# Swin-style window attention in four layers, one core: PE's order within an attention slot, and two queues for the first loads and the last stores

## The reference

```python
h = norm(x)                          # L0: over the whole image; L1 to L3: over the channels of a token
h = roll(h, (-3, -3)); windows of 7 x 7 = 49 tokens
q, k, v = h @ qkv_w + qkv_b          # 12 heads of 8 channels in L0 to L2, 4 heads of 24 in L3
a = softmax(q * hd**-0.5 @ k.T + rel_bias + mask)
x = x + roll(window_reverse(a @ v @ proj_w + proj_b), (3, 3))
x = x + mlp(norm(x))                 # 96 -> 384 -> 96, GELU between; L3 has one more norm on the 384
```

## Time and profile before

| what | value |
|---|---|
| median of 3 runs | 10196.03 us (10195.53 to 10201.48) |
| the profiled execution | 10191.26 us |
| its span on the core | 10189.4 us, so 1.9 us lie around it |
| mean granted clock of TensorE | 0.972 of full |
| PE busy | 87% of the span |
| PE weight loads busy | 64% |
| DVE / ACT / POOL busy | 67% / 54% / 50% |
| DMA | 57.27 MB, mean 6 GB/s |

### The profile page before, as it was taken

One profiled execution on the slowest core, in us unless ns is written; L12 is line 12 of the kernel. 1 busy time (PEld: TensorE's weight loads), 2 busy tenths in 40 slices (PEclk: granted clock), 3 DMA queues, 4 the chain that ended last, 5 costly groups with the idle time before them and its releaser, 6 DMA issues.

```text
span 10189.4 us, 315201 instructions
## 1 busy us (share of the span) xinstructions
PE 8861.1 (87%) x110128; PEld 6488.0 (64%) x110128; DVE 6823.7 (67%) x19999; ACT 5520.1 (54%) x9632; POOL 5091.5 (50%) x6190
## 2 busy tenths in 40 slices
PE   1899898998889899899888989989888998989984
PEld 0666666765667666666566667666556666667653
DVE  3766767657776666766867676666687667676574
ACT  0655646455564655646556464554556556464552
POOL 4764545443475554544257454554427645454431
PEclk8999999999999999999999999999999999999997
DMA  2010000000001000000000100000000000000000
GB/s 32 6 20 5 0 1 0 1 1 0 3 6 28 14 1 1 0 1 0 0 5 11 30 5 1 1 1 1 0 1 6 20 4 0 1 0 1 1 0 19
DMA packets 177574, 57.27 MB, mean 6 GB/s; under 512 B 175987, under 2 KB 177020, under 8 KB 177107
## 3 DMA queue, kind: packets, MB, share of 16 engines
q1 hardware_dynamic: 167768, 50.63, 2.8%
q0 software_dynamic: 4880, 0.71, 0.1%
q10 hardware_dynamic: 4459, 0.12, 0.1%
HBM read 31.71 MB, written 19.27 MB: 5 GB/s over the span
## 4 chain that ended last, share of the span: by engine, by line
issue 37%; POOL 21%; PE 20%; DVE 11%; ACT 4%; DVEq 3%; POOLq 3%; ACTq 0%; DMA 0%
POOL masked_bias L447 7%; POOL S L461 5%; PE ps L761 4%; PE ps L784 4%; PE ps L704 3%; POOL rstd L435 3%; ACT PT L574 3%; DVE xn L939 2%; POOL xn L478 2%; POOL xn L483 2%; DVE bst L849 2%; PE ps L746 2%; DVE bst L1049 2%; DVEq L939 2%; PE ps L668 1%
## 5 line engine op out<-in xcount | busy, mean ns | idle before, releaser
L461 POOL TENSOR_TENSOR S<-S,mx 113x588 f32<-113x588 f32 (+1 forms) x2048 | 2064.3, 1008 | 2618.8 <-DVE mx L988 2617.8
L704 PEld LDWEIGHTS ps<-Vroom,PT 98*49 98x49 f32 x40960 | 1123.4, 127 | 1365.3 <-ACT PT L574 1197.2
L574 ACT ACTIVATE PT<-ps 98x588 f32<-98x588 f32 (+1 forms) x2048 | 1179.4, 576 | 1490.9 <-PE ps L746 1456.5
L704 PE MATMUL ps<-Vroom,PT 98*49 98x18 f32 (+1 forms) x40960 | 1339.0, 203 | 651.7 <-ACT PT L574 628.4
L986 DVE TENSOR_TENSOR S<-ps,bias 113x588 f32<-113x588 f32 (+1 forms) x1536 | 973.4, 634 | 981.9 <-PE ps L690 915.0
L530 ACT ACTIVATE room<-ps,kmask 96x392 f32<-96x392 f32 x2048 | 1191.3, 583 | 578.3 <-PE ps L660 578.3
L988 DVE TENSOR_REDUCE mx<-S 113x12 f32<-113x588 f32 (+1 forms) x2048 | 1359.5, 664 | 70.7
L746 PE MATMUL ps<-ident,S 113*98 113x113 f32 x10240 | 1348.9, 262 | 2.4 <-ACT S L550 2.3
L550 ACT ACTIVATE S<-S 113x588 f32<-113x588 f32 (+1 forms) x2048 | 1238.4, 605 | 56.2 <-POOL S L461 56.2
L761 PEld LDWEIGHTS ps<-w,G 128*98 128x98 f32 x12288 | 1139.1, 168 | 112.8 <-issue 61.1
L746 PEld LDWEIGHTS ps<-ident,S 113*98 113x98 f32 x10240 | 1067.1, 129 | 197.4 <-issue 191.4
(11 more groups left out here) (81 smaller groups left out, 11852.9 us busy)
## 6 DMA issues: line engine op xcount, KB each, us to landing
mask<-L_conv_mask_matrix_dram SPq DMA_DIRECT2D x256, 37.5 KB
x<-x_dram SPq DMA_DIRECT2D x64, 84.0 KB
out_dram<-x SPq DMA_DIRECT2D x64, 84.0 KB
x<-x_dram SPq DMA_DIRECT2D x240, 10.5 KB
out_dram<-x SPq DMA_DIRECT2D x240, 10.5 KB
x<-x_dram SPq DMA_DIRECT2D x192, 18.4 KB
out_dram<-x SPq DMA_DIRECT2D x192, 18.4 KB
x<-x_dram SPq DMA_DIRECT2D x64, 48.0 KB
```

Of the source, the lines that this page charges most:

```text
L461: pool.tensor_tensor(v, v, m, ALU.subtract).then_inc(a_sub, 1)
L574: act.activation(PT[:, e, 0:blocks, :, :].rearrange("p (b t) w n -> p b (t w) n", b=banks), PTps[:, 0:banks, 0:2 * k, 0:N], ACT.Copy).then ...
L704: last = pe.matmul(Ops[ROW2 * w:ROW2 * w + N, p, b, :], PT[:, s % 2, b, w, :], room_of[:, o if s < 2 else t, p, w, b, :], start=True, stop ...
```

## The change

It has two parts.

1. In PE's `attend`, the weighted sums of pair s-2 move from before the projections of a slot to after them. The order in a slot is then scores, projection, weighted sums, turning.
2. The first 228 loads are issued first of all, every other one by SP and by ACT. The clearing of `x` is gone, and the waits on it. DVE takes the statistics of the first group before it writes the bias tables. The last group's stores are cut in two halves of two images, 156 DMAs each: SP issues the first half when 16 of the last stage's 32 quads are done, and SP and ACT issue every other one of the second half when the last quad is done.

```diff
-        def runs():
+        def runs(first, last):
...
-                    rows = [(slice(0, IMGS * A), r + SHIFT)]
+                    rows = [(slice(first * A, last * A), first * H + r + SHIFT)]
...
-        def tokens(sp, g, store, s):
+        def tokens(eng, g, store, s, first=0, last=IMGS, turn=0, turns=1):
...
+            for n, (q, a, j, row, col) in enumerate(runs(first, last)):
+                if n % turns != turn:
+                    continue
...
         @block.sync
...
             nc.disable_value_cache = True
+            tokens(sp, 0, False, s_x, turn=0, turns=2)
             load(ident[:, :], d["ident"])
...
-            sp.wait_ge(s_memset, 2)
-            tokens(sp, 0, False, s_x)
+            sp.wait_ge(s_memset, 1)
             load(mask4[:, :, :].rearrange("p a b -> p (a b)"), d["mask4"])
...
             sp.sem_inc(s_next, 1)
+            sp.wait_ge(m_res, GROUPS * LAYER_QUADS - NQ // 2)
+            stand(sp)
+            tokens(sp, GROUPS - 1, True, s_out, 0, IMGS // 2)
             sp.wait_ge(s_fin, GROUPS)
-            tokens(sp, GROUPS - 1, True, s_out)
-            sp.wait_ge(s_out, GROUPS * (16 * TOK_DMAS))
+            tokens(sp, GROUPS - 1, True, s_out, IMGS // 2, IMGS, turn=0, turns=2)
+            sp.wait_ge(s_out, (GROUPS - 1) * (16 * TOK_DMAS) + 2 * 16 * HALF_DMAS)
...
         @block.scalar
         def _(act):
-            act.wait_ge(s_memset, 2)
+            tokens(act, 0, False, s_x, turn=1, turns=2)
+            act.wait_ge(s_memset, 1)
             load_bias(act, 0, s_braw0)
...
+            act.wait_ge(s_fin, GROUPS)
+            tokens(act, GROUPS - 1, True, s_out, IMGS // 2, IMGS, turn=1, turns=2)
...
         @block.tensor
...
                                 last.then_inc(a_sc, 1)
-                            if on(-1) if s < 2 else on(0):
-                                wait(a_pte, before)
-                                p = (s + 2) % 4
...
                             if s == 0 and on(-2):
                                 wait(a_ote, i - 2)
...
                                 last.then_inc(a_t1, 1)
+                            if on(-1) if s < 2 else on(0):
+                                wait(a_pte, before)
+                                p = (s + 2) % 4
+                                if s == 2:
+                                    wait(a_o, i - 1)
+                                    wait(a_v0e, i)
+                                if s == 0:
+                                    wait(a_v2e, i - 1)
+                                room_of = Vbd if nh == 12 else Vbd3
+                                for b in range(blocks):
+                                    for w in range(2):
+                                        last = pe.matmul(Ops[ROW2 * w:ROW2 * w + N, p, b, :], PT[:, s % 2, b, w, :],
+                                                         room_of[:, o if s < 2 else t, p, w, b, :],
+                                                         start=True, stop=True)
+                                if s == 1:
+                                    last.then_inc(a_pv, 1)
                             if on(-1) if s == 0 else on(0):
                                 wait(a_pte, before)
                                 wait(a_exp, prior)
...
         @block.vector
         def _(dve):
-            dve.memset(x[:], 0.0).then_inc(s_memset, 1)
-            dve.wait_ge(s_memset, 2)
+            dve.wait_ge(s_memset, 1)
             dve.wait_ge(s_const, n_const[0])
+            dve.wait_ge(s_x, 16 * LOADS)
+            quad_steps(dve, 0, load_stats, 2)
             dve.wait_ge(s_braw, 16 * (LAYERS - 1) * WS * WS)
...
             dve.wait_ge(s_tab, LAYERS)
-            dve.wait_ge(s_x, 16 * LOADS)
-            quad_steps(dve, 0, load_stats, 2)
             with dve.Fori(0, GROUPS) as g:
```

More of the change, by code:

```diff
@@ L271, in runs @@
                 if r + SHIFT < WS:
-                    rows = [(slice(0, IMGS * A), r + SHIFT)]
+                    rows = [(slice(first * A, last * A), first * H + r + SHIFT)]
                 else:
-                    rows = [(slice(m * A, m * A + A - 1), m * H + r + SHIFT) for m in range(IMGS)]
-                    rows.append((slice(A - 1, IMGS * A, A), r + SHIFT - WS))
+                    rows = [(slice(m * A, m * A + A - 1), m * H + r + SHIFT) for m in range(first, last)]
+                    rows.append((slice(first * A + A - 1, last * A, A), first * H + r + SHIFT - WS))
                 for a, row in rows:
@@ L284, in runs @@
                                 yield slice(q + cut, q + WS), a, j, row, (col + cut) % W
-        def tokens(sp, g, store, s):
+        def tokens(eng, g, store, s, first=0, last=IMGS, turn=0, turns=1):
             dram = out if store else x_in
             rows_of = x[:, bass.ds((g % 2) * NP, NP), :].rearrange("p (a j) c -> p a j c", j=4)
-            n = 0
-            for q, a, j, row, col in runs():
+            for n, (q, a, j, row, col) in enumerate(runs(first, last)):
+                if n % turns != turn:
+                    continue
                 step = a.step or 1
@@ L297, in tokens @@
                 dst, src = (far, near) if store else (near, far)
-                sp.dma_start(dst, src).then_inc(s, 16)
-                n += 1
-            return n
+                eng.dma_start(dst, src).then_inc(s, 16)
         def mask_quad(sp, g, q, slot):
@@ L313, in mask_stream @@
                     mask_quad(sp, g, q + j, j)
-        TOK_DMAS = len(list(runs()))
+        TOK_DMAS = len(list(runs(0, IMGS)))
+        HALF_DMAS = len(list(runs(0, IMGS // 2)))
         LOADS = TOK_DMAS
@@ L406, in _ @@
             pool.memset(neghalf[:], -0.5).then_inc(s_memset, 1)
-            pool.wait_ge(s_memset, 2)
+            pool.wait_ge(s_memset, 1)
             for l in range(1, LAYERS):
@@ L880, in _ @@
             quad_steps(dve, 0, load_stats, 2)
+            dve.wait_ge(s_braw, 16 * (LAYERS - 1) * WS * WS)
+            dve.wait_ge(s_braw0, 16 * WS * WS)
+            dve.wait_ge(s_bsec, 16 * LAYERS)
+            for l in range(LAYERS):
+                nh = HEADS[l]
+                for v in range(1 if l == 0 else 4):
+                    for w in range(2):
+                        r = slice(ROW2 * w, ROW2 * w + N)
+                        dst = bias[l][r, v, :].rearrange("p (h k) -> p h k", k=N)
+                        src = stage(l)[r, :].rearrange("p (h k) -> p h k", k=N)[:, :, ::-1]
+                        if l == 0:
+                            last = dve.tensor_copy(dst, src)
+                        else:
+                            last = dve.tensor_tensor(dst, src, mask4[r, v, :].unsqueeze(1).to_broadcast([N, nh, N]),
+                                                     ALU.add)
+                last.then_inc(s_tab, 1)
+            dve.wait_ge(s_tab, LAYERS)
             with dve.Fori(0, GROUPS) as g:
```

## The result

The changed kernel is slower: median 11529.62 us of 4 runs against 10195.78, and the ratio is 1.1166, 95% interval [1.1139, 1.1192]. I had forecast 9965 us. The four runs are 11381.70, 11385.85, 11673.40 and 11944.00 us; the ratio rests on the two lowest, since the others are over 1.5% above them.

What follows compares the result with a forecast made beforehand. PE's ordered blocks and waits were taken to bound the kernel. From 10191.3 us it subtracted 84 (12-head quads), 13 (layer 3), 60 (start) and 72 (end), 229 in all: 9962, median of runs about 9965; range 9840 to 10075.

Steps and rivals of the forecast that it cites:

- wait at the weighted sums goes: PE's wait for ACT's copy of the turned probabilities vanishes: 1.63 us a quad, 626 us over 384 quads.
- new wait at L721: start after T1: Slot 3: the outputs' turning waits 0.90 us for ACT's key copy, starting 2.07 + 0.04 after pair 1's turning.
- turning behind the weighted sums: Each slot: turning the probabilities right after the weighted sums takes 0.71 us instead of 0.67, +0.04.
- whole block ahead of the weighted sums: Each slot: leaving the whole-array shape for column halves costs about 0.09 us, bounds 0 and 0.25.
- 12-head quad: Attention quads of the 12-head layers take 13.18 us, a gain of 0.22 each, 84 us over 384 quads.
- layer-3 quad: Layer 3's attention quads gain 0.1 us each, between 0 and 0.22, 13 us over 128 quads.
- start: Loads split between SP and ACT let DVE begin at about 92 us instead of 154.94; gain taken as 60 us.
- end: Stores after the last quad, split over two queues, gain 65 to 78 us, taken as 72.
- A: Attention: leaving a whole block for halves costs nothing; a 12-head quad takes 12.82 us, total 9777 us; chance 0.15.
- B: Attention stays as it was, shape changes eating the wait's gain; only start and end gain: 10059 us; chance 0.22.
- D: Start and end: two queues share one rate; start gains 0, end 37 us, total 10057 us; chance 0.05.
- C: Slower: weighted sums behind a projection cost 0.25 us a slot instead of 0.09, 328 us more: 10290 us; chance 0.05.

Runs made afterwards that it cites:

- (2): The kernel before with only PE's new order; loads, statistics and stores as before: 11491.79 us, ratio 1.1266.
- run 3: `quad0_fill`: the changed kernel plus one dummy matmul in slot 3 of quads 0 and 1 of each attention stage: 9970.72 us, ratio 0.9776.
- run 5: `key_early`: the changed kernel with ACT's fourth key copy made before its copy of the turned probabilities: 11399.50 us.
- run 7: Three kernels without the dummy matmuls ahead of and in each attention stage's first quad: new order 14256.74 us, old order 10847.83, old in slot 3 only 10890.78.
- nobusy_slot3: Third kernel of run 7: new order in slots 0 to 2, old in slot 3, without the dummy matmuls at each attention stage's start: 10890.78 us.
- turn_first: The changed kernel with the slot order scores, projection, turning, weighted sums: 10261.50 us, ratio 1.0067.
- key_fill: The changed kernel with the fourth key copy early and the dummy matmul in slot 3 of quads 0 and 1: 9752.40 us, ratio 0.9566.

## Why the prediction was wrong

**What failed** is a step that the prediction does not even name: it summed PE's blocks at the durations of the earlier trace rows, all of them at the full clock, as if the order could not change the clock. The profile of before had the warning. Its windows in the stage at 5172 us:

```profile
5172.00:5184.00 12.00, 11.41 (x155) 7.10 (x154) 7.17 (x10) 6.89 (x13) 8.14 (x7) 1.00 0.04 6
5184.00:5194.00 10.00, 9.42 (x89) 6.81 (x84) 4.55 (x7) 4.06 (x8) 6.63 (x6) 0.55 0.01 2
5194.00:5208.00 14.00, 12.74 (x208) 9.28 (x206) 8.65 (x13) 9.33 (x16) 8.65 (x8) 0.96 0.04 8
```

The clock fell there for 10.2 us, in 3 of 12 stages, and came back by itself. Its rise on PE's timeline:

```profile
5190.35 2.92 PE L660 MATMUL ps<-hT,wqkv 97*96 97x392 f32 x4
5193.08 1.34 PE L746 MATMUL ps<-ident,S 113*98 113x113 f32 x6
5194.34 0.94 PE L690 MATMUL ps<-room,QT 32*64 32x196 f32 x12
5195.34 0.73 PE L704 MATMUL ps<-Vroom,PT 98*49 98x18 f32 x24
```

The clock is back at 5195.15, after a projection with the turning right behind it, two whole-array blocks in a row. In the new order the weighted sums stand between these two in every slot, and none of the five falls in the changed kernel (0.50 for 685 to 689 us each) ended before the last scores of its stage. Shown by runs: the order alone traps the stages (2), a fall avoided leaves about the forecast time (3), the new slot-3 wait is not the cause (5), the old order rises from half clock and the new one doesn't, and one slot in the old order is enough (both 7).

What in the order does it is argued from the traces. In all fourteen traces together the clock rises 83 times between the first and the last scores of a 12-head stage, and each time 0.8 to 2.2 us after the start of a turning that directly follows the slot's projection step. The steady quads of the new order have no such place; the only two rises in it are in the first quad of a stage, before there are weighted sums. The length of a run of whole-array blocks does not explain it: at half clock the new order has 2.91 us of them in slot 0 (output projection and values, 1011.61 to 1014.52 in the changed kernel) and no rise, and slot 3 of the third kernel of run 7 has 2.70 us (1585.39 to 1588.09) and rises. Layer 3, whose turning is two transposes and not six, does not rise from half clock in any of the three orders of run 7; its scores have another shape too. Whether it matters that the second block is transposes was not separated, and what sets the granted clock was not shown; that stays open.

How busy PE is in the profile does not decide it by itself. The falls at or up to 2.5 us behind a wait of 1.10 us, and the dummies of run 3, with which no attention stage is trapped, would fit that; the stage of run 5 does not, with PE busy in 660.00 of 660 us at 0.50.

**The other steps**, by their sizes (from the warm stages and from `quad0_fill`):

| step | forecast | measured |
|---|---|---|
| wait at the weighted sums goes | 1.63 us a quad | gone |
| new wait at L721: start after T1 | 2.07 + 0.04 | 2.11 |
| turning behind the weighted sums | +0.04 | +0.05 (0.72 for 0.67) |
| whole block ahead of the weighted sums | +0.09 (0 to 0.25) | +0.09 |
| 12-head quad | 13.18 | 13.15 |
| layer-3 quad | gain 0.1 | 0.12 |
| start | 60 | 40 (first norm at 182.85 for 223.09) |
| end | 72 | 72 (48 us after the last add, for 119) |
| all, at the full clock | 9965 | 9970.72 (`quad0_fill`, with its dummies) |

The order's gain is thus some 0.24 x 384 + 0.12 x 128 = 108 us of the 626 that the wait's total promises. The rest went to the wait at L721 (0.82 us in the quad above) and to the blocks on both sides of the weighted sums, where one more change of array shape stands in each slot: 0.09 and 0.05 us, 0.14 in all for the 0.13 of the forecast. That the change of shape is what costs them is my reading; no run separates it from the order of the blocks. The start was mis-sized: I took 0.554 us an issue for each of two queues, and they took 0.74; my lower case of 0.685 was the nearer one.

That the whole comes within 6 us of the forecast is in part luck. By span, `quad0_fill` gains 41 us ahead of the first scores, 107 in the attention stages and 72 behind the last of them, where I had 60, 97 and 72: the start fell 19 us short of my sum, and attention gave 10 more.

Rivals A and B (other prices for the change of shape) and D (one rate for both queues) fell. So did C: the kernel is slower, but not by its mechanism, since the price that it put at 0.25 is 0.09. No rival touched the clock, and the chance of 0.05 for a slower kernel rested on C alone. Two of the prediction's own signs of being wrong came: a quad over 13.4 us (22.56 in the trapped stages), and statistics that start after 110 us (117.77).

## What to carry to other kernels

Before reordering PE, look where the granted clock falls in the old trace and what stands in front of each rise, and whether the new order still has such a place: here the sum of warm durations, 9965 us, was met where no attention stage was trapped (9970.72, `quad0_fill`) and missed by 1565 us where five or more were. Test an order cold: take away the warm-up matmuls, and see whether steady work brings the clock back. And when a wait is to be filled, ask what is tied to another engine behind it: here the key copy, hidden by 0.09 us, took back 0.86 us a quad of the 1.10 that the new order gains without it in layer 0 (13.39 to 12.29).

## What the runs showed of the hardware that was not expected

- One and the same loop ran at one of two clocks, 1.00 or 0.50, for a whole stage: 13.15 us or 22.56 us a quad, in stages of 413 and 699 us, with PE busy for over 93% of the time in both (383.62 of 410 us, 646.09 of 659). In the changed kernel it was decided within 13 us of the first scores.
- Whether a half clock ended went with the order of the same blocks, not only with how much PE did in a given time: at half clock a quad of `key_early` takes 22.06 us and stays low, one of `nobusy_slot3` takes 21.89 us and rises.
- A short wait of PE was followed by a fall: 1.10 us in 5 of 8 stages of the changed kernel, 0.59 to 0.98 us (0.79 at the median) ahead of the 48 falls inside the stages of `turn_first`. But 0.50 us in most quads of layers 1 and 2 of `key_fill` trapped no stage.
- A 12-head quad of the changed kernel at half the clock takes 1.72 times as long (22.56 / 13.15), not twice.
- The queues of SP and ACT, issuing these loads at once, took 0.74 us for each, against 0.554 when SP alone issued them (ACT issued 49 other loads beside it, and POOL others in both kernels): 1.5 times the rate, not twice. At the end, with PE, ACT and POOL idle (0.00 us busy from 11332 to 11379), two took 0.58 (45.32 / 78) against 0.517.
